# One VectorE multiply over two PSUM banks instead of two multiplies over one bank each, with item banks taken in fixed pairs

## What is computed

```python
# e: (2048, 40, 64), one row of each of 40 embedding tables per sample, fp32
p, q = e[:, rowidx], e[:, colidx]          # all 780 pairs i < j of fields
z = einsum('bie,fie,bif->bi', p, param, q) # param: (64, 780, 64)
h = relu(concat([z, dense_ctx]) @ W_top1 + b_top1)   # 796 -> 512
h = relu(h @ W_top2 + b_top2)                        # 512 -> 256
y = h @ W_top3                                       # 256 -> 1
```

## Time and profile before

| | |
|---|---|
| Time, median of 3 runs | 1218.11 us (1217.02 to 1220.1) |
| Span of the profiled execution | 1255.3 us |
| PE busy | 1224.6 us (98%) |
| DVE busy | 1053.7 us (84%) |
| ACT busy | 972.3 us (77%) |
| Mean granted TensorE clock | 0.989 |

### The profile page before, as it was taken

The page is one execution under the profiler, slowest core; times in us unless marked ns, Lnnn a source line. Parts: engine busy times, 40 slices in busy tenths (PEclk is TensorE's granted clock), DMA queues, the critical chain, the costliest instruction groups (busy, mean ns, idle before and its releaser), DMA issues.

```text
span 1255.3 us, 22898 instructions
## 1 busy us (share of the span) xinstructions
PE 1224.6 (98%) x5808; PEld 476.8 (38%) x5808; DVE 1053.7 (84%) x1720; ACT 972.3 (77%) x7177; POOL 573.2 (46%) x607
## 2 busy tenths in 40 slices
PE   6989999999999999999999999999999999999999
PEld 3323433333333333333333433334333334333333
DVE  6858899988888797889998888788999878899980
ACT  0019999975868887898968988799968988899951
POOL 5655554455455555555245555555245555400000
PEclk9988899999999999999999999999999999999999
DMA  7033344433544333333454433333353434122100
GB/s 207 18 113 104 79 119 117 110 104 92 140 100 120 102 104 87 88 81 97 106 134 106 113 84 94 87 80 96 95 155 90 114 97 111 49 63 83 44 1 1
DMA packets 132098, 118.87 MB, mean 95 GB/s; under 512 B 91351, under 2 KB 110039, under 8 KB 131965
## 3 DMA queue, kind: packets, MB, share of 16 engines
q1 hardware_dynamic: 111188, 94.94, 27.3%
q0 software_dynamic: 19200, 19.70, 7.6%
q10 hardware_dynamic: 1576, 2.76, 0.8%
HBM read 80.09 MB, written 0.01 MB: 64 GB/s over the span
## 4 chain that ended last, share of the span: by engine, by line
PE 88%; ACT 7%; issue 2%; DVE 2%; DMA 1%; SPq 0%; ACTq 0%; DVEq 0%
PE ring L793 40%; PE z_ps L816 18%; PE ring L798 17%; PE ring L822 8%; ACT wide_prod L606 6%; PE ring L756 2%; PE ring L826 2%; DVE prod L671 1%; DMA z_t<-tbl 1%; DVE wide_prod L685 0%; ACT e_t L567 0%; PE ring L774 0%; PE ring L829 0%; ACT h L620 0%; PE ring L767 0%
## 5 line engine op out<-in xcount | busy, mean ns | idle before, releaser
L606 ACT ACTIVATE wide_prod<-wide_prod 128x64 f32<-128x64 f32 x3520 | 841.8, 242 | 55.1 <-DVE wide_prod L685 34.8
L537 POOL DMA_INDIRECT rows<-tbl,idx_now x600 | 572.4, 954 | 514.9 <-DMA rows<-tbl,idx_now 310.0
L671 DVE TENSOR_TENSOR prod<-ring,e_t 128x512 f32<-128x512 f32 x1008 | 630.6, 683 | 114.3 <-PE ring L793 97.0
L606 ACT ACTIVATION_READ_ACCUMULATOR wide_prod<-wide_prod 128x1 f32 x3520 | 662.6, 188 | 17.8 <-issue 17.1
L793 PE MATMUL ring<-e_t,w 64*128 64x512 f32 x2176 | 584.3, 613 | 13.6 <-issue 4.8
L685 DVE TENSOR_TENSOR wide_prod<-ring,rows 128x512 f32<-128x512 f32 x512 | 327.8, 682 | 32.1 <-PE ring L798 12.8
L793 PEld LDWEIGHTS ring<-e_t,w 64*128 64x128 f32 x2176 | 229.0, 187 | 326.0 <-issue 210.0
L798 PE MATMUL ring<-w,e_t 64*128 64x512 f32 x1024 | 305.8, 616 | 4.2 <-DVE wide_prod L685 1.8
L816 PE MATMUL z_ps<-prod,strip 128*32 128x512 f32 x2096 | 253.9, 598 | 0.0
L798 PEld LDWEIGHTS ring<-w,e_t 64*128 64x128 f32 x1024 | 116.2, 189 | 150.5 <-issue 85.9
L816 PEld LDWEIGHTS z_ps<-prod,strip 128*32 128x32 f32 x2096 | 55.0, 109 | 179.7 <-issue 117.0
(11 more groups left out here) (24 smaller groups left out, 76.4 us busy)
## 6 DMA issues: line engine op xcount, KB each, us to landing
w<-weights SPq DMA_DIRECT2D x64, 768.0 KB
planes<-words SPq DMA_DIRECT2D x284, 64.0 KB
rows<-tbl,idx_now POOLq DMA_INDIRECT x600
z_t<-tbl SPq DMA_DIRECT2D x10, 224.0 KB
w<-weights SPq DMA_DIRECT2D x4, 512.0 KB
w<-hot_ids ACTq DMA_DIRECT2D x7, 256.0 KB
w<-w1z SPq DMA_DIRECT2D x7, 256.0 KB
words<-rows SPq DMA_TRANSPOSE x71
```

Source lines behind the costliest of these rows:

```text
L537: nc.gpsimd.indirect_dma_start(out=fields([tile], slice(slot, slot + 1), t)[:, 0, f, :], out_offset=None, in_=tables[m * 2 + f], in_offset ...
L606: last = nc.scalar.activation(products, products, ACT.Copy, accum_out=z_b[:, h, t, col:col + 1])
L671: nc.vector.tensor_tensor(dst[:, j, :], ring[:, bank, :], e_t[:, k, :], ALU.mult).then_inc(t_free, 1)
```

## The change

Units off the diagonal and wide items get one DVE multiply over both banks (two times 512 columns, the second operand repeated for both) in place of two over one each. For that the two banks of an item must be neighbours: items take the pairs (0,1), (2,3), (4,5) in turn, and all other takers have bank 6 alone (before the first item and after the last, banks are dealt out in rotation). DVE waits for both matmuls of the item (`through(n)`, which is 2n + 2) before its one multiply, and adds one to `t_free`, not two; diagonal units keep two multiplies and two counts. `FREED[n]` is the count after item n, and whoever waited for an item's banks now waits for `FREED[n]`: PE too, which before waited for each bank's own multiply.

```diff
+PAIRS = 3
+SINGLE = 6
...
+def on_diagonal(item):
+    _, kind, i = item
+    return kind == "unit" and UNITS[i][0] == UNITS[i][1]
+
+FREED = list(itertools.accumulate(2 if on_diagonal(item) else 1 for item in ITEMS))
...
 def bank_plan():
-    takers = []
+    taken = []
+    pairs = 0
     for n in range(ALL_ITEMS):
-        takers += [("tile", t) for t in TILES_AT.get(n, ()) if not by_dma(t)]
+        singles = [("tile", t) for t in TILES_AT.get(n, ()) if not by_dma(t)]
...
-        takers += [("item", n)] * 2
...
+        for taker in singles:
+            taken.append((taker, SINGLE if pairs else len(taken) % RING))
+        for half in range(2):
+            taken.append((("item", n), 2 * (pairs % PAIRS) + half))
+        pairs += 1
...
+    taken += [(taker, (SINGLE + i) % RING) for i, taker in enumerate(tail)]
...
+        def both(banks):
+            return ring[:, banks[0]:banks[0] + 2, :]
+
+        def runs_of_rows(c, t):
+            fixed = rows[:, fixed_slot(c):fixed_slot(c) + FIXED, :]
+            if by_dma(c * TILES):
+                runs = fixed.rearrange("p k (f t e) -> p (k f) t e", f=2, t=BT)[:, :, t, :]
+            else:
+                runs = fixed.rearrange("p k (t f e) -> p k t (f e)", f=2, t=BT)[:, :, t, :]
+            return runs.unsqueeze(1).broadcast_to([P, 2, *runs.shape[1:]])
...
             def unit(n, c, u):
-                for j, bank in enumerate(banks):
-                    dve.wait_ge(t_ready, 2 * n + j + 1)
-                    if k == m:
+                if k == m:
+                    for j, bank in enumerate(banks):
+                        dve.wait_ge(t_ready, 2 * n + j + 1)
...
-                    else:
-                        nc.vector.tensor_tensor(dst[:, j, :], ring[:, bank, :], e_t[:, k, :],
-                                                ALU.mult).then_inc(t_free, 1)
+                else:
+                    dve.wait_ge(t_ready, through(n))
+                    nc.vector.tensor_tensor(dst, both(banks), e_t[:, k:k + 1, :].broadcast_to([P, 2, NB]),
+                                            ALU.mult).then_inc(t_free, 1)
...
             def wide(n, c, v):
-                for j, bank in enumerate(BANKS["item", n]):
-                    dve.wait_ge(t_ready, 2 * n + j + 1)
-                    nc.vector.tensor_tensor(dst[:, j, :, :, :], src[:, bank, :, :, :],
-                                            fields(fixed, slice(fixed_slot(c), fixed_slot(c) + FIXED), t),
-                                            ALU.mult).then_inc(t_free, 1)
+                dve.wait_ge(t_ready, through(n))
+                runs = runs_of_rows(c, t)
+                length = runs.shape[-1]
+                nc.vector.tensor_tensor(
+                    wide_prod[:, number % WIDE_SLOTS, :, :].rearrange("p j (q e) -> p j q e", e=length),
+                    both(BANKS["item", n]).rearrange("p j (q e) -> p j q e", e=length),
+                    runs, ALU.mult).then_inc(t_free, 1)
...
             def take_bank(taker, i=0):
...
-                        pe.wait_ge(t_free, 2 * n + BANKS[before].index(bank) + 1)
+                        pe.wait_ge(t_free, FREED[n])
```

More of the change, by code:

```diff
@@ L1 @@
+import itertools
 from contextlib import ExitStack
@@ L307, in bank_plan @@
 def bank_plan():
-    takers = []
+    taken = []
+    pairs = 0
     for n in range(ALL_ITEMS):
-        takers += [("tile", t) for t in TILES_AT.get(n, ()) if not by_dma(t)]
+        singles = [("tile", t) for t in TILES_AT.get(n, ()) if not by_dma(t)]
         if n in STEPS_AT:
             c, s = STEPS_AT[n]
-            takers.append(("step", c * STEPS + s))
+            singles.append(("step", c * STEPS + s))
         if n in TURNS_AT:
-            takers.append(("turn", TURNS_AT[n]))
-        takers += [("item", n)] * 2
-    takers.append(("step", (CHUNKS - 1) * STEPS))
-    takers += [("turn", h) for h in range(HALVES_ALL) if turn_at(h) >= ALL_ITEMS]
-    takers += [("step", (CHUNKS - 1) * STEPS + s) for s in range(1, STEPS)]
+            singles.append(("turn", TURNS_AT[n]))
+        for taker in singles:
[3 more added lines that the diff above has]
+        pairs += 1
+    tail = [("step", (CHUNKS - 1) * STEPS)]
+    tail += [("turn", h) for h in range(HALVES_ALL) if turn_at(h) >= ALL_ITEMS]
+    tail += [("step", (CHUNKS - 1) * STEPS + s) for s in range(1, STEPS)]
+    taken += [(taker, (SINGLE + i) % RING) for i, taker in enumerate(tail)]
     banks, before, owner = {}, {}, [None] * RING
[L323 to L326, removed]
+    for taker, bank in taken:
+        banks.setdefault(taker, []).append(bank)
+        before.setdefault(taker, []).append(owner[bank])
+        owner[bank] = taker
     return banks, before
@@ L524, in _ @@
                 if m < FIXED and use > 1:
-                    pool.wait_ge(t_free, through(PLACE[c - 2, "wide", NW - 1]))
+                    pool.wait_ge(t_free, FREED[PLACE[c - 2, "wide", NW - 1]])
                 elif use > 1:
@@ L559, in prepare @@
                 if c > 0:
-                    act.wait_ge(t_free, through(last_reader(c - 1, m)))
+                    act.wait_ge(t_free, FREED[last_reader(c - 1, m)])
                 if by_dma(tile):
@@ L600, in reduce @@
                     act.wait_ge(turned, (c - 1) * HALVES + h + 1)
-                act.wait_ge(t_free, through(PLACE[c, "wide", v]))
+                act.wait_ge(t_free, FREED[PLACE[c, "wide", v]])
                 for jj in range(2):
@@ L679, in wide @@
                     wait_reduced(dve, number - WIDE_SLOTS + 1)
-                dst = wide_prod[:, number % WIDE_SLOTS, :, :].rearrange("p j (k f e) -> p j k f e", k=FIXED, f=2)
-                src = ring[:, :, :].rearrange("p b (k f e) -> p b k f e", k=FIXED, f=2)
-                fixed = [c * TILES + k for k in range(FIXED)]
-                for j, bank in enumerate(BANKS["item", n]):
-                    dve.wait_ge(t_ready, 2 * n + j + 1)
-                    nc.vector.tensor_tensor(dst[:, j, :, :, :], src[:, bank, :, :, :],
-                                            fields(fixed, slice(fixed_slot(c), fixed_slot(c) + FIXED), t),
-                                            ALU.mult).then_inc(t_free, 1)
+                dve.wait_ge(t_ready, through(n))
[5 more added lines that the diff above has]
+                    runs, ALU.mult).then_inc(t_free, 1)
             def reduce(n, c, v):
@@ L694, in reduce @@
                     dve.wait_ge(turned, (c - 1) * HALVES + h + 1)
-                dve.wait_ge(t_free, through(n))
+                dve.wait_ge(t_free, FREED[n])
                 nc.vector.tensor_reduce(z_b[:, h, t, first:first + WIDE_PAIRS],
@@ L808, in sum_group @@
                     pe.wait_ge(z_copied, Z_NUMBER[before] + 1)
-                pe.wait_ge(t_free, through(last_of_group(group)))
+                pe.wait_ge(t_free, FREED[last_of_group(group)])
                 first, end = GROUP_FIRST[Z_FIRST[t]], GROUP_FIRST[Z_FIRST[t + 1]]
```

## The result

The changed kernel takes 1250.70 us (median of 4, 1246.05 to 1255.52); the kernel before, beside it, 1218.16 us (median of 4, 1217.02 to 1220.1). The ratio is 1.0239 with a 95% interval from 1.0179 to 1.0299: slower by 32.5 us. The forecast was 1248 us, 30 us slower.

What follows compares the result with a forecast made beforehand. PE's own pace bounds runs of five, with PE and DVE matched in runs of six. Longer runs, 28.5 us, plus 2 us for diagonal units give 30 us on 1218: 1248 us, range 1212 to 1270.

Steps and rivals of the forecast that it cites:

- The merged multiply: On DVE: one multiply 1.21 us long, 1.13 apart, saves 0.065 us an item, 49 us of DVE's time.
- the 1.19 us behind its 1257: Alternative spacing of merged multiplies: pairs come free at 2.50, 3.69 and 4.88 us, and the time is about 1257 us.
- The release of three pairs: PE's item n + 3 waits for item n's whole multiply: runs of five 0.2 us longer, six 0.4; together 28.5 us.
- wait for both halves: DVE's wait for both matmuls of an item: they run side by side on PE, so it costs nothing.
- DVE's idle time at the group: At every group three full pairs last 3.4 us against 4.04 us to bridge, so DVE idles some 0.6 us.
- diagonal units: Among a run's first items, one delays a release by 0.2 to 0.3 us; some 10 of 40, 2 us.
- Reductions: DVE's 36 reductions push releases by 1.13 us in both kernels; taken as nothing, between -5 and +10.
- DVE is the bound: Rival: 49 us less DVE work come off the end; 1202 us, or 1169 if all of it; chance 0.14.
- the point at which it decides: Run length where 0.065 us an item outweighs DVE's idle 0.6 us and more at its end: above ten items.
- It comes to nothing: Rival: with spacing 1.07 waits are short and longer runs and reductions give the gain back; 1218 to 1222 us; chance 0.10.
- Late counts in the timed runs too: Rival: DVE starts late in timed runs too, runs of five lose 0.47 us, not 0.2; 1265 us; chance 0.08.
- The merged multiply saves nothing: Rival: 1.28 us long, 1.20 apart; runs of five lose 0.35 us, six 0.61; 47 us, 1265 us; chance 0.08.

Runs made afterwards that it cites:

- pairs_apart: Fixed pairs and bank 6 for all others as in the changed kernel, but two multiplies per item as in the kernel before: 1260.0 us, ratio 1.0327.
- merge_last: Kernel before, seven banks in rotation, one multiply only for 381 items among the last three before PE is interrupted: 1220.74 us, ratio 1.0007.
- light_merged: Changed kernel with half of each group's sums and three of four later gathers left out: 1146.37 us; same cuts with separate multiplies: 1160.91 us.
- merge_first: Kernel before, seven banks in rotation, one multiply only for 273 items with three or more behind them in their run: 1243.83 us, ratio 1.0186.

## Why the prediction held, step by step

**The merged multiply.** Taken as 1.21 us long and 1.13 apart; measured 1.217 and 1.13. DVE's busy time fell from 1050.9 to 1003.2 us. The page "Perfetto Trace Analysis" of the Trainium skill, section "Optimizing Scalar/DVE Operations", puts the overhead on PSUM at about 125 ns an instruction; for 760 instructions fewer that is an estimate of 95 us. The trace shows half of it, as the row of the reduction had promised. The prediction's two figures by that page don't go together: 95 us less is a spacing of 1.20 - 0.125 = 1.075 us, near its own lower bound of 1.07, while the 1.19 us behind its 1257 fits 2 x 0.53 + 0.125, by which two separate multiplies would lie 1.31 us apart and not 1.20. Nothing in the sum rests on them.

**The release of three pairs** decided it, as said. Runs of five got 0.25 us longer (0.2 predicted; 6.60 us against 6.55), runs of six 0.45 (0.4; 7.72 against 7.68), runs of four nothing. The mis-sized term is a small one. The first multiply of a run starts 1.27 us after the first matmul (621.41 - 620.14), not 1.23. The traces put these 0.04 us down to the merged multiply with its wait for both halves, which the prediction took at nothing. Behind the first 150 us, counting the runs whose first multiply finds DVE idle, all 97 that begin with a merged unit show 1.27, the 10 that begin with a unit on the diagonal, which waits for one half, show 1.23, and in `pairs_apart` all that begin with a unit show 1.23. Whether the wait or the longer instruction is at fault isn't told apart. They push every release. Pairs come free 3.68 and 4.81 us into the run (1.27 + 1.13 + 1.22 + 0.06, and 1.13 later) instead of 3.63 and 4.76, and item 6 of the run above does begin at 4.81. Runs of seven got 0.45 longer, not 0.3: both kernels were slower there than counted, 8.71 and 9.16 us with the group against 8.5 and 8.8. The three in the table each have a unit on the diagonal as third item. The only run of seven without such a unit, at 261.5 us in the second profile of before, comes to 6.61 + 1.85 = 8.46 and 7.00 + 1.85 = 8.85 us, close to the count.

**DVE's idle time at the group** was put at 0.6 us and is 0.84. The count 3 x 1.13 = 3.4 us took three full pairs to begin with the last item's matmul; but that matmul waits until the pair is free, and DVE began the next multiply 0.14 us earlier (0.08 of overlap and 0.06 to the matmul). 1.27 + 1.85 + 0.96 = 4.08 us less 3.39 - 0.14 = 3.25 leaves 0.83. This doesn't enter the sum.

**The total.** 28.5 predicted for the runs, 33.4 by the table; 30 with the diagonal units, 32.5 measured. The rest may be the late tiles, which hid 35.0 - 32.5 = 2.5 us, within what these medians can tell. Diagonal units can be read from the same two traces: between 350 and 1215 us seven runs of five have one as first or second item, and each takes 5.01 or 5.02 us in the changed kernel and 4.49 in before. That is 0.27 more than the other runs of five lose, within the 0.2 to 0.3 predicted. Reductions gave a little back, as was thought possible: in six of the runs that follow one, a reduction cost the old kernel 0.5 us (5.01 instead of 4.49, three runs) or 0.4 (5.84 instead of 5.42, three), and the changed kernel only 0.2 (4.93 and 6.04), some 1.7 us in all.

**The rivals.** *DVE is the bound* fell twice: `merge_last` saves DVE time for nothing, and the change is slower. But the point at which it decides was real, and `light_merged` lies beyond it. The same section of the Trainium skill says, for an engine that isn't saturated but causes bubbles on others, that breaking up instructions may let work be completed sooner. In the rotation this agrees with the runs: splitting the 273 items of `merge_first` gives 22 us. In fixed pairs it doesn't: `pairs_apart`, with everything split, is slower than the changed kernel by 9 us. *It comes to nothing* needed a spacing of 1.07. *Late counts in the timed runs too* fell with the second profile of before. *The merged multiply saves nothing* is `pairs_apart`: 1265 counted, 1260.0 measured.

**What was wrong.** "A profiled span of about 1285": it is 1253.7. The working counted on the first profile's lateness to recur in that of the changed kernel; it belonged to that execution alone. The time was not touched by this, since the differences were taken run by run from undisturbed rows and added to the median. That 30 and 32.5 us lie so close is in part luck: by the medians the runs were counted some 5 us too cheap (28.5 against 33.4), and the late tiles of the old kernel took about half of that off again. And the prediction looked for no third bound: late tiles, which that disturbed profile covered, stood behind PE in the old kernel.

## What to carry to other kernels

Merging two instructions also merges the release of their buffers. Before doing it, ask for each buffer whether the producer wants it back before its next pause: where it doesn't, the merge is free (and here worth nothing), and where it does, the later release can cost more than the saved overhead. If the profiled execution is 3% longer than the timed median, take another profile before reading bounds from it.

## What was not expected of the hardware

One execution of the kernel before had a span of 1255.3 us where a second profile of the same kernel had 1217.3. The granted clock was 0.989 and 0.990, so it doesn't tell them apart. The difference sat in multiplies that began long after their matmuls had ended, 1.8 us in the earlier trace rows, in runs that otherwise take 6.34 us. Behind the first 150 us, of the runs whose first multiply found DVE idle, 55 of 109 began it more than 1.35 us after their first matmul, up to 3.86. In the second profile of before none of 102 did (1.23 to 1.35), in that of the changed kernel none of 136 (1.23 to 1.30). No run here shows what delays such a count.
